# Ordering TensorE's work in an attention kernel: score tiles in runs of three, three and two, weighings in pairs, a job behind each other run

## The reference

```
attn = softmax(q k^T / 4)                        # per batch, head
coh  = sigmoid(tanh([x, cond] Wc1^T + bc1) Wc2^T + bc2)
mod  = attn * coh ;  mod = mod / (sum(mod) + 1e-8)
mod  = 0.79 * mod + 0.21 * fa                    # fa: softmax over positions, one row per batch
y    = x + (mod v) Wout^T + bout
out  = y + quaternion_map(y)                     # left and right Hamilton products, a gate
```

## Time and profile before

| | |
|---|---|
| time, median of 3 runs | 307.48 us (306.29 to 308.24) |
| span of the profiled execution, first to last instruction | 302.4 us |
| PE busy | 272.4 us, 90% |
| DVE busy | 197.7 us, 65% |
| ACT busy | 176.2 us, 58% |
| POOL busy | 157.9 us, 52% |

### The profile page before, as it was taken

The page is one execution under the profiler, slowest core; times in us unless marked ns, Lnnn a source line. Parts: engine busy times, 40 slices in busy tenths (PEclk is TensorE's granted clock), DMA queues, the critical chain, the costliest instruction groups (busy, mean ns, idle before and its releaser), DMA issues.

```text
span 302.4 us, 4278 instructions
## 1 busy us (share of the span) xinstructions
PE 272.4 (90%) x1579; PEld 130.0 (43%) x1579; DVE 197.7 (65%) x227; ACT 176.2 (58%) x214; POOL 157.9 (52%) x143
## 2 busy tenths in 40 slices
PE   8999397598979999999899999999999988899973
PEld 6447244233534444444444454446444433344422
DVE  6485355556777677887577668785876778864113
ACT  3224034456667768676448677674667666655760
POOL 3933639998199999993003069960000399900000
PEclk9999687989999999999999999999999999999999
DMA  7717839739773934399318933695159500101002
GB/s 240 214 44 217 192 53 121 175 61 120 138 245 52 125 37 152 98 117 173 126 69 109 109 83 122 96 121 171 54 86 121 90 2 4 33 3 69 1 0 72
DMA packets 16020, 31.11 MB, mean 103 GB/s; under 512 B 2232, under 2 KB 8248, under 8 KB 14656
## 3 DMA queue, kind: packets, MB, share of 16 engines
q1 hardware_dynamic: 15168, 30.15, 50.9%
q10 hardware_dynamic: 832, 0.69, 0.8%
HBM read 20.21 MB, written 10.49 MB: 102 GB/s over the span
## 4 chain that ended last, share of the span: by engine, by line
PE 59%; DVE 18%; DMA 13%; issue 4%; SPq 2%; POOL 1%; ACT 1%; DVEq 0%; ACTq 0%; POOLq 0%
PE o_ps L1018 15%; DVE maxima L660 14%; PE job_ps L794 12%; PE pair_ps L990 11%; PE pair_ps L1003 9%; DMA stack<-qk_scratch 6%; PE job_ps L908 4%; DMA stack<-max_rows 3%; DVE qk_lo L676 2%; DMA w_raw<-wqkvT 2%; DMA qk_scratch<-qk_lo 2%; SPq L313 1%; PE pair_ps L882 1%; PE job_ps L849 1%; PE pair_ps L794 1%
## 5 line engine op out<-in xcount | busy, mean ns | idle before, releaser
L660 DVE TENSOR_REDUCE maxima<-pair_ps 128x2 f32<-128x1024 f32 x128 | 155.5, 1222 | 69.1 <-PE pair_ps L990 69.1
L513 ACT ACTIVATE probs<-pair_ps 128x1024 f32<-128x1024 f32 x128 | 130.8, 1025 | 65.6 <-PE pair_ps L1003 64.9
L990 PE MATMUL pair_ps<-stack 48*128 48x512 f32 x256 | 64.5, 500 | 8.2 <-DMA stack<-qk_scratch 7.6
L1018 PE MATMUL o_ps<-probs,vals 128*32 128x512 f32 x512 | 69.0, 612 | 0.8 <-ACT probs L513 0.8
L1003 PE MATMUL pair_ps<-stack 49*128 49x512 f32 x256 | 57.1, 444 | 9.8 <-DVE maxima L660 7.0
L990 PEld LDWEIGHTS pair_ps<-stack 48*128 48x128 f32 x256 | 24.2, 186 | 56.9 <-issue 40.0
L389 POOL TENSOR_TENSOR vals<-v_new,row 128x256 f32<-128x256 f32 x16 | 11.3, 733 | 48.5 <-ACT v_new L545 48.2
L1003 PEld LDWEIGHTS pair_ps<-stack 49*128 49x128 f32 x256 | 24.4, 187 | 28.3 <-DVE maxima L660 18.8
L488 POOL TENSOR_TENSOR prod<-amap,x_tok 128x1024 f32<-128x1024 f32 x12 | 28.6, 2382 | 0.9
L372 POOL TENSOR_TENSOR x_lo<-x_raw,x_hi 128x1024 fp32r<-128x1024 f32 x3 | 7.1, 2375 | 32.9 <-ACT x_hi L519 32.8
L490 POOL TENSOR_TENSOR y<-y,prod 128x1024 f32<-128x1024 f32 x8 | 19.1, 2382 | 0.6
(11 more groups left out here) (134 smaller groups left out, 297.2 us busy)
## 6 DMA issues: line engine op xcount, KB each, us to landing
stack<-qk_scratch SPq DMA_DIRECT2D x42, 256.0 KB, 8.9
qk_scratch<-qk_hi SPq DMA_DIRECT2D x16, 256.0 KB, 5.4
qk_scratch<-qk_lo SPq DMA_DIRECT2D x16, 256.0 KB, 5.8
x_tok<-x SPq DMA_DIRECT2D x4, 512.0 KB, 14.3
out<-y SPq DMA_DIRECT2D x8, 256.0 KB, 2.2
x_raw<-xT SPq DMA_DIRECT2D x3, 512.0 KB, 5.9
fa_now<-fa_rows SPq DMA_DIRECT2D x4, 256.0 KB, 7.7
stack<-qk_scratch SPq DMA_DIRECT2D x6, 128.0 KB, 4.7
```

The source lines that it names most:

```text
L513: nc.scalar.activation(probs[:, t % 4, :, :], ps[:, :, :], ACT.Exp, scale=SCALE).then_inc(exp_done, 1)
L660: nc.vector.tensor_reduce(maxima[:, gg % 2, :, pair, i], pair_ps[SLOT["S", u]][:, :, :], AX_X, ALU.max, negate=True).then_inc(s_reduced, 1)
L990: ins = nc.tensor.matmul(pair_ps[SLOT["S", u]][:, a, :], stack[64 * a:64 * a + ROWS, 0, p, i * P:(i + 1) * P], stack[64 * a:64 * a + ROWS, ...
L1018: ins = nc.tensor.matmul(o_ps[h * VW:(h + 1) * VW, :], vals[:, j, gg % G * HG + h, :], probs[:, (2 * k + h // 2) % 4, h % 2, :], start=(j ...
```

## The change

The 32 steps of a batch become 8 groups of four steps, called quads (`QUAD`). From step 12 on, the four S and four T tiles of a quad stand in runs: S T S, then two W and a small job (part 0: max, z, zt or field), then T S T, a job (part 1), then S T, a job (part 2). The plan of all engines comes from one list (`plan`, `PLAN`). The first twelve steps and the end, behind step 127, keep their order, but one W (number 56) stands ahead of the end.

- The W of a quad are the two whose last exponential is of the quad before. `probs` holds six T tiles instead of four (`RING`); the two new places share their memory with `w_dir` and `dir_part`, which only the start uses.
- q0, q1, v0 and coh0 use the bank `o_ps` between two groups of W (`ON_O`). They wait until ACT has copied `o_ps` out (`groups_weighed`), and the first W of the next group waits until they have been read (`job_before_group`). The other jobs stay in `job_ps`.
- v1 of a batch stands in the last quad of the batch before, not at its step 10, and q0 and k0, q1 and k1, coh0 and coh1 stand in one quad each.

The diff, cut to its core:

```diff
+RING = 6
...
+QUAD = 4
+JOB_QUADS = {"q0": (-5, 1), "k0": (-5, 2), "q1": (-3, 1), "k1": (-3, 2), "v0": (-1, 1), "v1": (-1, 2),
+             "coh0": (1, 1), "coh1": (1, 2), "max0": (2, 0), "z": (3, 0), "max1": (4, 0), "zt": (5, 0), "max2": (6, 0),
+             "field": (7, 0), "max3": (8, 0), "tok0": (6, 1), "tok1": (8, 1), "tok2": (10, 1), "tok3": (12, 1),
+             "back0": (12, 2), "back1": (14, 2), "out0": (16, 2), "out1": (18, 2)}
...
+ON_O = ("q0", "q1", "v0", "coh0")
...
+    for quad in range(LEAD // QUAD, STEPS // QUAD):
+        run = [(kind, n - lag) for n in range(QUAD * quad, QUAD * (quad + 1)) for kind, lag in (("S", 0), ("T", LEAD))]
+        k = 2 * (quad - LEAD // QUAD - 1)
+        order += run[0:3] + [("W", n) for n in (k, k + 1) if k >= 0] + [("J", job) for job in jobs.get((quad, 0), [])]
+        order += run[3:6] + [("J", job) for job in jobs.get((quad, 1), [])]
+        order += run[6:8] + [("J", job) for job in jobs.get((quad, 2), [])]
...
-                    wait(act, av_done, t // 2 - 1)
+                    wait(act, av_done, t // 2 - RING // 2 + 1)
...
             def claim(job):
                 if before_in_bank(job):
                     wait(pe, *read_out(before_in_bank(job)))
+                if PLACE[job] >= EARLY and bank_of(job) == 1:
+                    wait(pe, o_raw_done, groups_weighed(job))
...
                 if j == 0:
                     pe.wait_ge(v_ready, gg + 1)
-                    if gg:
-                        pe.wait_ge(o_raw_done, gg)
-                    else:
-                        pe.wait_ge(*read_out(last_early(1)))
+                    wait(pe, o_raw_done, gg)
+                    if job_before_group(gg):
+                        pe.wait_ge(*read_out(job_before_group(gg)))
```

More of the change, by code:

```diff
@@ L51, with jobs_by_place @@
 LATE = ("q0", "q1", "k0", "k1", "out0", "out1")
-def jobs_by_step():
+def jobs_by_place():
     table = {}
     for b in range(B):
-        steps = {**JOB_STEPS, **(FIRST_STEPS if b == 0 else LAST_STEPS if b == B - 1 else {})}
-        for name, step in steps.items():
-            if b == 0 and name in BEFORE:
+        places = {**JOB_QUADS, **(FIRST_QUADS if b == 0 else THIRD_QUADS if b == B - 2 else {})}
+        for name, (quad, part) in places.items():
+            n = QUADS * b + quad
+            if b == 0 and name in (*BEFORE, *FIRST_STEPS) or b == B - 1 and name in TAIL_STEPS:
@@ L60, in jobs_by_step @@
                 continue
-            table.setdefault(PER_BATCH * b + step, []).append((name, b))
+            table.setdefault((n, part), []).append((name, b))
     return table
-JOBS = jobs_by_step()
-LAST_STEP = max(JOBS)
-ORDER = [(name, 0) for name in BEFORE] + [job for n in range(LAST_STEP + 1) for job in JOBS.get(n, [])]
-PLACE = {job: n for n, job in enumerate(ORDER)}
[L71 to L84, removed]
@@ L89 @@
+PLAN = plan()
+ORDER = [job for kind, job in PLAN if kind == "J" and job[0] != "fore"]
+PLACE = {job: n for n, job in enumerate(ORDER)}
+EVENTS = [(kind, n) for kind, n in PLAN if kind in "ST"]
 ALONE = len(EVENTS) - LEAD
@@ L94, with bank_of, groups_weighed, job_before_group @@
          for n, event in enumerate(EVENTS)}
+def bank_of(job):
+    if PLACE[job] < EARLY:
+        return PLACE[job] % 4
+    return 1 if job[0] in ON_O else 0
 def before_in_bank(job):
[L99 to L102, removed]
+    same = [other for other in ORDER[:PLACE[job]] if bank_of(other) == bank_of(job)]
+    return same[-1] if same else None
 def last_early(bank):
     return ORDER[max(n for n in range(EARLY) if n % 4 == bank)]
+def groups_weighed(job):
+    return sum(kind == "W" and k % IT == IT - 1 for kind, k in PLAN[:PLAN.index(("J", job))])
+def job_before_group(gg):
+    first = PLAN.index(("W", IT * gg))
+    since = PLAN.index(("W", IT * gg - 1)) if gg else 0
+    return next((job for kind, job in reversed(PLAN[since:first])
+                 if kind == "J" and job[0] != "fore" and bank_of(job) == 1), None)
 ROW_BV, ROW_BOUT, ROW_Q, ROW_GATE, ROW_END = 0, 256, 512, 1024, 1088
@@ L639, in _ @@
             act.wait_ge(ld_col, 16)
[L640 to L643, removed]
+            for kind, n in PLAN:
+                if kind == "S" and n % PER_BATCH == 4 and n // PER_BATCH < B - 1:
                     x_high(n // PER_BATCH + 1)
[L645 to L651, removed]
+                elif kind == "T":
+                    exponentials(n)
+                elif kind == "W" and n % IT == IT - 1 and n // IT != G * B - 2:
+                    attention_out(n // IT)
+                elif kind == "J":
+                    evacuate(n)
         @block.vector
@@ L768, in _ @@
             dve.wait_ge(ld_col, 16)
[L769 to L772, removed]
+            held = None
+            for kind, n in PLAN:
+                if kind == "S":
                     reduce_scores(n)
[L774 to L784, removed]
+                elif kind == "W" and n == IT * (G * B - 1) - 1:
+                    attention_out(n // IT)
+                if held and kind in "SJ":
+                    evacuate(held)
+                    held = None
+                if kind == "J" and n[0] in LATE:
+                    held = n
+                elif kind == "J":
+                    evacuate(n)
+            evacuate(held)
         @block.tensor
```

62 lines of the change are left out of this document (36 added, 26 removed).

## The result

| | before | after |
|---|---|---|
| time, median | 306.88 us (305.84 to 308.24) | 336.16 us (334.70 to 338.45) |
| span of the profiled execution | 302.4 us | 334.0 us |
| mean granted clock in it | 0.977 | 0.908 |

A forecast was written before the change was run, and what follows sets the result against it. TensorE's order was taken to set the pace. Floor plus buffer waits gave stretches of 32.2, 63.8, 61.5 and 57.5, together 215.0 against 218.1; span 299.3 plus 5.1 made 304.3 us, 1.0% faster, range 297.5 to 311.

The forecast's parts named there:

- SP's reads and writes keep their order; v1's and k's earlier places only advance them.: SP's queue: claimed that the change delays none of its reads or writes; no cost was entered.
- C: T tiles at quad starts: the maxima's DMA lands late at three further places, +7.0, time 311.4; chance 0.15.
- unchanged in number: Floor of each stretch: same jobs as before, 22.4 us in batch 2, 14.3 in batch 3, 7.6 in the first.
- the 2.3 for the maxima: Batch 1: a T tile waits 2.3 us for the maxima's DMA, on top of the 3.7 of other waits.
- The only cold term: First stretch: W 0 and 1 run cold after a longer idle time, costing 1.7 us.
- Runs of three: PE's tiles in a quad: three tiles without another kind between cost 0.92 us, against 0.68 for two.
- the S tile behind tok: Fourth S of a quad with max, tok and back: waits 0.6 us for a T tile's exponential to free its buffer.
- rival A: All stretches: waits stay as they were and only the floor falls, by 5.8 us; time 301.7, chance 0.22.
- B: Run edges on PE cost the same in any order, so 6.8 us of edges stay; time 311.1, chance 0.10.
- D: Projections into `o_ps` wait for ACT's late copy, 0.5 at 14 places, +7, time 311; chance 0.08.
- The ring of six costs nothing: `probs`: an exponential waits only for the first W of its own quad, issued ahead, so no cost was entered.
- The 5.1 us between span and median: Whole kernel: 5.1 us added to the forecast span of 299.3 to give the time.

The follow-up runs named there:

- e1: The changed kernel with SP's read of the next operands ahead of the store of the batch before; 309.06 us, ratio 1.0173 to the kernel before.
- e3: The kernel before with one more wait on SP, so the operand reads for S tiles 80 and 112 go out late; 328.23 us, ratio 1.0784.
- e9: e1 with out0 of the third batch in `o_ps` instead of `job_ps`; 305.07 us, ratio 0.9922 to the kernel before.
- e11: e10 plus three unread matmuls in each of seven empty parts of quads; 300.14 us, ratio 0.9751 to the kernel before.
- e6: e1 with tiles in runs of two, each W by itself and all jobs in `job_ps`; 314.05 us, ratio 1.0113 to the kernel before.
- e5: e1 with the small job of a quad ahead of the two W instead of behind; 319.07 us, ratio 1.0357 to the kernel before.
- e8: e5 with out0 of the third batch in `o_ps` and four places in `probs` instead of six; 328.05 us, no ratio.
- e2: The changed kernel with out0 and out1 of every batch in quad 15 of their batch, SP untouched; 316.40 us, ratio 1.0429 to the kernel before.
- e10: e9 with 22 unread matmuls at the end of quad 3, ahead of S tile 16; 305.92 us, ratio 0.9858 to the kernel before.
- e12: The kernel before with 10 unread matmuls behind the W of step 15; 306.96 us, ratio 0.997.

## Why the prediction was wrong

1. **The step that failed** is the sentence "SP's reads and writes keep their order; v1's and k's earlier places only advance them." The order is kept, but I looked for jobs that moved forward and read no queue for those that moved back. out1 of batches 0 and 1 moved by 13 steps, and the store that waits for it has the next operands' read behind it in SP's queue. Price, as e1 takes it back: 12.4 + 14.7 us in two stretches, waits of 10.4 and 12.7 and the low clock behind them; e3 brings most of it into the old order. No rival had it: C asked for late maxima, which go by ACT's queue, and the range ended at 311.

2. **The same oversight in the sum.** I kept the jobs of each stretch "unchanged in number". But batch 0's outs left batch 1 and batch 1's came into batch 3, 1.9 us each (176.55 to 178.44). Together e1's four stretches take 221.7 for a forecast of 215.0: 3.6 over in the first, 3.5 under in batch 1, 0.4 under in batch 2, 7.0 over in batch 3. In e1, where the queue is out of the way, batch 1 takes 60.3 for a forecast of 63.8: 3.8 of outs and the 2.3 for the maxima are not there, 1.4 of a W pair on the low clock is extra, and the remaining 1.2 I put down to waits in the quads left empty. Batch 3 takes 64.5 for 57.5. Its two quads with outs of batch 1 take 7.8 instead of the 6.8 I gave them, 2.1 together. The last one takes 13.6 with W 56 for a forecast of 9.8: 1.8 is out1's wait for the bank and 1.6 its low clock (e9 removes both). One more quad, with a W pair of 2.85, has 1.8 too much, and the other four are 0.7 quicker together.

3. **Waits were priced once, and the clock charges them again.** The only cold term was 1.7 for W 0 and 1. In e1 the W pairs of quads 4 and 5 take 3.57 and 3.42 for 1.85, 3.3 over, so 1.6 of the 3.6 that this stretch is over (35.8 for 32.2) is the second pair; the rest is not taken apart. e11 bears it out from the other side: with the waits filled the kernel is 1.7% quicker than e9 (0.9751 against 0.9922). The size is not a rule, since the same waits did not always bring the low clock.

4. **What held.** Runs of three 0.91 (forecast 0.92); W pairs 1.85 (1.90, bounds 1.80 to 2.00); the S tile behind tok waits 0.3 to 0.5 (0.6), so rival A is out by its own sign; the next quad's T follows its S by 0.63; batch 2, the one stretch with a clock of 1.00 and no outs moved across its ends in number, takes 61.1 in e1 for 61.5, though A's sum would have given 60.65 (63.05 - 2.4), about as near. B is out by the 0.91 and by e6's 4.1 us (its time should read 311.2, which changes nothing). D is out: no projection into `o_ps` shows a wait for ACT. C came at one place in batch 0, in some executions only (about 1.0 of the 1.64 in the first section, 1.78 in e9, nothing in e1), instead of in batch 1, where the wait of the earlier trace rows is gone.

5. **The ring of six costs nothing**: no wait in the changed kernel's list speaks against it, but I had not asked what it brings, nor what the W pair covers. e5's eight waits of about 1.5 show the second, e8 hints at the first.

6. **Span and time.** The 5.1 us between span and median that I took as fixed are not: in the changed kernel's profiled execution 1.8 lie around the span (335.8 against 334.0). The rest of the 5.1 I put down to a profiled execution that was quicker than the median. It cancels in the difference of 3.1 us, and decides nothing here.

## What to carry to other kernels

For each job that a change moves, also the ones moved back, follow its output to every queue that waits for it in order, and read what stands behind the waiting instruction: here a store that nobody needs held a read that everybody needs. Put loads ahead of stores in one queue. In a stretch bound by TensorE, price a cluster of short waits as time and as a possible low clock behind it, and look at what a moved block had covered.

## What the runs showed of the hardware

- The granted clock fell to 0.50 behind waits of 0.48, 0.17 and 0.64 us in a row (e2, 165 to 168), and behind one of 1.64 (82.37). It did not fall behind the same waits in quad 18 of e2 and once in e1 (114.0 to 118.7, at 1.00). In the kernel before, with PE busy for 8.24 of the 10 us from 82 on, it stayed at 1.00. The Trainium skill, "TensorE: Matmul & The Clock Gate", section "A second HAM failure mode: psum-queue depth-cycling", says that short idle times between groups of matmuls, as they cycle through PSUM, can make the clock swing between its levels; these rows agree, and show that they need not.
- With three matmuls that nobody reads in each of seven places where TensorE waits, the clock was 1.00 where it had been 0.97, and the work added paid for itself (e11). A longer fill at the start could not be told from nothing (e10, e12).
- A busy PE is no proof of a quick one: 9.63 us of 10 at clock 0.50 held 41 matmuls, and 8.24 at 1.00 held 60.
- The read of six pieces that landed unnoticed in the kernel before took some 15 us from its issue at 181.39 to the tile at 196.85, with a DMA share of 1.00 from 184 to 197. It had 25 us before.
- A store that waits for its data holds a read queued behind it on SP, with the transfer engines nearly free: from 165.16 to 181.39 SP stood at the second store, and the DMA share from 165 to 181 was 0.05.
